# The product of Q with the carried state in 32x32 tiles into attention banks that ScalarE seeds, with statistics in steps and turns without loops

## What is computed

```
q = elu(x @ Wq.T + bq) + 1        # 16 heads of 32 features
k = elu(x @ Wk.T + bk) + 1
v = x @ Wv.T + bv
kv_cum = cumsum(k (outer) v, over tokens);  k_cum = cumsum(k)
out = (q . kv_cum) / max(q . k_cum, 1e-6)
y = out @ Wo.T + bo
...
second layer: blocks of 32 features scaled by their largest value and rounded
to an 8 bit grid, times the weight treated alike, + bias
```

## Time and profile before

| | us |
|---|---|
| median of 3 runs | 2538.85 (2538.05 to 2539.38) |
| the profiled execution | 2537.71 |
| its span, first to last instruction | 2535.9 |
| TensorE busy | 2475.8 (98%), 24082 records |
| VectorE busy | 2088.7 (82%) |
| ScalarE, GpSimd busy | 1139.3 (45%), 994.5 (39%) |
| TensorE's share of the chain that ended last | 86% |

### The profile page before, as it was taken

The page is one execution under the profiler, slowest core; times in us unless marked ns, Lnnn a source line. Parts: engine busy times, 40 slices in busy tenths (PEclk is TensorE's granted clock), DMA queues, the critical chain, the costliest instruction groups (busy, mean ns, idle before and its releaser), DMA issues.

```text
span 2535.9 us, 62336 instructions
## 1 busy us (share of the span) xinstructions
PE 2475.8 (98%) x24082; PEld 2058.8 (81%) x24082; DVE 2088.7 (82%) x4177; ACT 1139.3 (45%) x2058; POOL 994.5 (39%) x1482
## 2 busy tenths in 40 slices
PE   6999999999999999999999999999999999999996
PEld 4888888888888888888888888888888888888885
DVE  6888888888888888888888888888888888888875
ACT  4444445444444444454444454444444444544442
POOL 1233344343344343443433443434443334434334
PEclk8999999999999999999999999999999999999998
DMA  4011011110111110111110111101111101111001
GB/s 157 14 51 49 17 41 50 41 50 25 41 41 41 50 50 17 41 50 41 50 34 33 41 43 48 50 17 41 50 41 50 46 20 41 50 41 50 25 26 34
DMA packets 57483, 107.55 MB, mean 42 GB/s; under 512 B 6768, under 2 KB 7152, under 8 KB 56816
## 3 DMA queue, kind: packets, MB, share of 16 engines
q1 hardware_dynamic: 57456, 107.18, 12.8%
HBM read 73.60 MB, written 33.55 MB: 42 GB/s over the span
## 4 chain that ended last, share of the span: by engine, by line
PE 86%; DVE 8%; ACT 3%; issue 2%; DMA 1%; POOL 0%; DVEq 0%; POOLq 0%; SPq 0%
PE work L345 14%; PE work L347 13%; PE work L346 13%; PE score L345 9%; PE score L347 9%; PE score L346 9%; PE work L362 6%; PE score L436 4%; PE work L462 4%; DVE A L878 3%; PE work L455 2%; PE work L411 1%; PE state_bank L477 1%; ACT xn L599 1%; DVE oT_lo L885 1%
## 5 line engine op out<-in xcount | busy, mean ns | idle before, releaser
L878 DVE TENSOR_TENSOR A<-score,causal 128x512 f32<-128x512 f32 x512 | 316.8, 680 | 0.6 <-PE score L436 0.6
L1063 POOL TENSOR_TENSOR x_res<-x_res,o_buf 128x512 f32<-128x512 f32 x128 | 166.3, 1299 | 294.2 <-ACT o_buf L599 294.2
L1053 POOL TENSOR_TENSOR rs_f<-ve_f,minus_half 128x1 f32<-128x1 f32 x128 | 70.3, 549 | 419.8 <-DVE ve_f L797 419.8
L345 PE MATMUL work<-wv_hi,xT_hi 128*128 128x512 f32 x512 | 215.3, 420 | 0.0
L345 PE MATMUL score<-xT_hi,wq_hi 128*128 128x512 f32 x512 | 207.1, 404 | 7.3 <-DVE KT L816 7.3
L345 PE MATMUL score<-xT_hi,wk_hi 128*128 128x512 f32 x512 | 206.4, 403 | 6.2 <-issue 6.2
L345 PE MATMUL work<-wo_hi,oT_hi 128*128 128x512 f32 x512 | 202.7, 396 | 2.2 <-DVE oT_lo L885 1.9
L1072 POOL TENSOR_TENSOR xd<-q,xs 128x512 f32<-128x512 fp8e4 x128 | 148.3, 1159 | 137.6 <-PE work L362 137.6
L347 PE MATMUL work<-wv_hi,xT_lo 128*128 128x512 f32 x512 | 201.0, 393 | 0.0
L346 PE MATMUL score<-xT_lo,wq_hi 128*128 128x512 f32 x512 | 200.7, 392 | 0.0
L346 PE MATMUL work<-wv_lo,xT_hi 128*128 128x512 f32 x512 | 200.5, 392 | 0.0
(11 more groups left out here) (130 smaller groups left out, 6523.4 us busy)
## 6 DMA issues: line engine op xcount, KB each, us to landing
x_in<-in_x SPq DMA_DIRECT2D x128, 256.0 KB, 3.5
x_res<-in_x SPq DMA_DIRECT2D x128, 256.0 KB, 2.6
out<-f_buf SPq DMA_DIRECT2D x96, 256.0 KB, 2.0
out<-xd SPq DMA_DIRECT2D x32, 256.0 KB, 2.0
V<-in_wk SPq DMA_DIRECT2D x1, 1024.0 KB, 6.0
QT<-in_wq SPq DMA_DIRECT2D x1, 1024.0 KB, 7.5
kc<-in_wo SPq DMA_DIRECT2D x1, 1024.0 KB, 9.4
A<-in_wf SPq DMA_DIRECT2D x1, 1024.0 KB, 11.4
```

The costliest lines, as they stand in the source:

```text
L345: nc.tensor.matmul(dst, st_hi(c), mv_hi(c), start=(c == 0), stop=False)
L878: nc.vector.tensor_tensor(A[:, j, :, :], score_bank[j][:], causal[:].unsqueeze(1).to_broadcast([P, G, P]), ALU.mult).then_inc(a_set, 1)
L1053: nc.gpsimd.tensor_tensor(rs[n][:, b:b + 1], ve[n][:, b:b + 1], minus_half[:], ALU.pow).then_inc(rs_set[n], 1)
L1063: nc.gpsimd.tensor_tensor(x_res[:, b, :], x_res[:, b, :], o_buf[:, b % 2, :], ALU.add).then_inc(r_set, 1)
```

## The change

`attend` loses its four state matmuls. Instead `past_products` makes, once a turn after v(1), the product of Q with the state for all four b in 64 products of 32x32 weights: the rows of head j, the columns of group g, so 16 places of the array, into `score_bank[j]`. S now holds only the 32x32 blocks and is one copy a turn (`state` on ScalarE). ScalarE copies the four score banks into `past_att` (`past`), and writes for each b the att bank from it (`seed`), on which `attend` then accumulates. Heads in the attention output stand in another order, and the rows of Wo are laid out to match on the host. att is always in work bank 2. v(2) and v(3) now stand in front of the attention of b 0. The statistics are three functions (`x_seen` and its like, `join`, `widen`), as are the steps of quantise (`greatest`, `scale`, `quantise`), and stand apart with other work between; the carry copies are ScalarE's (`carry`). The loops are replaced by turns written out. ScalarE's, VectorE's and GpSimd's lists within a turn are reordered.

```diff
-    (("f", 2), W2), (("xd", 3), W1), (("den", 0), W0), (("v", 0), W2), (("kn", 0), W1), (("f", 3), W0),
-    (("v", 1), W1), (("x", 0), W2), (("att", 0), W0), (("kn", 1), W2),
-    (("v", 2), W1), (("o", 0), W2), (("x", 1), W0), (("att", 1), W1), (("kn", 2), W0),
-    (("v", 3), W2), (("o", 1), W0), (("x", 2), W1), (("att", 2), W2), (("kn", 3), W1),
-    (("x", 3), W0), (("o", 2), W1), (("att", 3), W0),
+    (("f", 2), W2), (("xd", 3), W1), (("v", 0), W0), (("den", 0), W2), (("kn", 0), W1), (("f", 3), W0),
+    (("v", 1), W1), (("v", 2), W2), (("v", 3), W0), (("x", 0), W1), (("att", 0), W2),
+    (("kn", 1), W0), (("o", 0), W1), (("x", 1), W0), (("att", 1), W2),
+    (("kn", 2), W1), (("o", 1), W0), (("x", 2), W1), (("att", 2), W2),
+    (("kn", 3), W0), (("x", 3), W1), (("o", 2), W0), (("att", 3), W2),
...
-        S = sb("S", [P, NSEQ, G, P])
+        S = sb("S", [P, NSEQ, G, DH])
+        past_att = sb("past_att", [P, NSEQ, HPG, P])
...
-            with sp.Fori(1, TILES - 1) as i:
+            for i in range(1, TILES - 1):
...
-                            pe.wait_ge(qn_set, count(i, 3))
+                            pe.wait_ge(past_set, count(i, HPG - 1))
...
-                def attend(b):
-                    if cur:
-                        take(i, ("att", b), here, before)
+                def past_products():
+                    if cur:
                         if first:
                             pe.wait_ge(state_zeroed, 1)
                         else:
-                            pe.wait_ge(s_set, count(i - 1, b))
-                        att = by_group(bank(("att", b))[:])
-                        for g in range(G):
-                            nc.tensor.matmul(att[:, g, :], S[:, b, g, :], QT[:, g, b * P:(b + 1) * P],
-                                             start=(g == 0), stop=False, skip_group_check=True)
+                            pe.wait_ge(s_set, count(i - 1, 0, 1))
+                        wait_apart(pe, qn_set, count(i, 3))
+                        for b in range(NSEQ):
+                            for g in range(G):
+                                for j in range(HPG):
+                                    rows = slice(j * DH, (j + 1) * DH)
+                                    last = nc.tensor.matmul(score_bank[j][g * DH:(g + 1) * DH, b, :], S[rows, b, g, :],
+                                                            QT[rows, g, b * P:(b + 1) * P], start=True, stop=True)
+                        last.then_inc(past_mm, 1)
+                def attend(b):
+                    if cur:
                         pe.wait_ge(a_set, count(i, b * HPG + HPG - 1, 16))
                         pe.wait_ge(v_set, count(i, b))
-                        for g in range(G):
-                            for j in range(HPG):
+                        pe.wait_ge(seeded, count(i, b))
+                        att = by_group(bank(("att", b))[:])
+                        for j in range(HPG):
+                            for g in range(G):
                                 feats = slice((g * HPG + j) * DH, (g * HPG + j + 1) * DH)
-                                last = nc.tensor.matmul(att[j * DH:(j + 1) * DH, g, :], V[:, b, feats],
+                                last = nc.tensor.matmul(att[g * DH:(g + 1) * DH, j, :], V[:, b, feats],
                                                         A[:, j, g, :], start=False, stop=True,
...
-                        if b > 0:
-                            pe.wait_ge(s_set, count(i, b - 1))
-                        elif not first:
-                            pe.wait_ge(s_set, count(i - 1, NSEQ - 1))
+                        if b == 0 and not first:
+                            pe.wait_ge(s_set, count(i - 1, 0, 1))
...
+                v(0)
                 denominators()
-                v(0)
                 kn(0)
+                f(3)
                 spread()
-                f(3)
+                v(1)
+                past_products()
+                v(2)
                 scores(0)
-                v(1)
+                v(3)
                 x_transposes(0)
                 attend(0)
                 state(0)
                 kn(1)
                 scores(1)
-                v(2)
                 if cur:
                     o(i, 0)
...
+                def carry(g):
+                    if cur:
+                        act.wait_ge(scanned, count(i, g))
+                        nc.scalar.copy(KT[:, g, :, CARRY], kc[:, g, :, SEG - 1]).then_inc(kc_set, 1)
...
-                def state(b):
-                    if cur:
-                        act.wait_ge(st_mm, count(i, b))
-                        for j in range(HPG):
-                            rows = slice(j * DH, (j + 1) * DH)
-                            last = nc.scalar.copy(S[rows, b, :, rows], state_bank[rows, b, :, :])
-                        last.then_inc(s_set, 1)
+                def past(j):
+                    if cur:
+                        act.wait_ge(past_mm, count(i, 0, 1))
+                        nc.scalar.copy(past_att[:, :, j, :], score_bank[j][:]).then_inc(past_set, 1)
+                def seed(b):
+                    if cur:
+                        take(act, i, ("att", b), {0}, set())
+                        if b == 0:
+                            act.wait_ge(past_set, count(i, HPG - 1))
+                        nc.scalar.copy(bank(("att", b))[:],
+                                       past_att[:, b, :, :].rearrange("p j t -> p (j t)")).then_inc(seeded, 1)
+                def state():
+                    if cur:
+                        act.wait_ge(st_mm, count(i, NSEQ - 1))
+                        nc.scalar.copy(S[:], state_bank[:]).then_inc(s_set, 1)
...
-            def stats(tile, n, b, src):
-                nc.vector.bn_stats(bn[n][:, b, :], src).then_inc(seen[n], 1)
+            def join(tile, n, b):
+                if n == "x" and not (isinstance(tile, int) and tile == 0):
+                    dve.wait_ge(rstd_set[n], count(tile - 1, b))
                 wait_apart(dve, seen[n], count(tile, b))
                 nc.vector.bn_aggr(mv[n][:, b, :], bn[n][:, b, :]).then_inc(joined[n], 1)
+            def widen(tile, n, b):
                 dve.wait_ge(joined[n], count(tile, b))
                 nc.vector.tensor_scalar(ve[n][:, b:b + 1], mv[n][:, b, 1:2], LN_EPS, None,
                                         ALU.add).then_inc(var_set[n], 1)
...
-                        dve.wait_ge(scanned, count(i, g))
-                        nc.vector.tensor_copy(KT[:, g, :, CARRY], kc[:, g, :, SEG - 1]).then_inc(kc_set, 1)
...
+    def by_head_in_group(w):
+        return np.ascontiguousarray(np.asarray(w).T.reshape(G, HPG, DH, D).transpose(0, 2, 1, 3).reshape(P, HPG, D))
```

More of the change, by code:

```diff
@@ L259, in had_before, with take @@
             return None
+        def take(engine, i, stage, here, before):
+            found = had_before(stage, here, before)
+            if found is None:
+                return
+            other, turns = found
+            reader, per = freed[other[0]]
+            engine.wait_ge(reader, count(i + turns + tile_of(other), other[1], per))
         def tokens(t, g):
@@ L333, in _ @@
         def _(pe):
[L334 to L341, removed]
             def product3(dst, st_hi, st_lo, mv_hi, mv_lo):
@@ L396, in v @@
                     if cur:
-                        take(i, ("v", b), here, before)
+                        take(pe, i, ("v", b), here, before)
+                        if first and b == 0:
+                            pe.wait_ge(wf_lo_set, G)
                         weights(i, "v")
@@ L402, in denominators @@
                     if cur:
-                        take(i, ("den", 0), here, before)
+                        take(pe, i, ("den", 0), here, before)
                         if first:
-                            pe.wait_ge(wf_lo_set, G)
                             pe.wait_ge(small_loaded, 16 * N_SMALL)
@@ L483, in x_transposes @@
                     if nxt:
-                        take(i, ("x", b), here, before)
+                        take(pe, i, ("x", b), here, before)
                         pe.wait_ge(xn_set, count(i + 1, b))
@@ L488, in o @@
                 def o(tile, b):
-                    take(i, ("o", b), here, before)
+                    take(pe, i, ("o", b), here, before)
                     pe.wait_ge(oT_set, count(tile, b))
@@ L495, in xd_transposes @@
                     if prev:
-                        take(i, ("xd", b), here, before)
+                        take(pe, i, ("xd", b), here, before)
                         pe.wait_ge(xd_set, count(i - 1, b))
@@ L501, in f @@
                     if prev:
-                        take(i, ("f", b), here, before)
+                        take(pe, i, ("f", b), here, before)
                         pe.wait_ge(xdT_set, count(i - 1, b))
@@ L573, in _ @@
             turn(0, {0, 1}, {1})
-            with pe.Fori(1, TILES - 1) as i:
+            for i in range(1, TILES - 1):
```

(56 more changed lines are left out.)

231 lines of the change are left out of this document (151 added, 80 removed).

## The result

The changed kernel takes **2466.7 us** (median of 4 runs, 2466.4 to 2468.8), the kernel before on the same chip 2538.5: ratio 0.972, 95% interval 0.970 to 0.974. The forecast was 2453, its range 2443 to 2490: right in sign and range, 13.7 us too low in size, and 0.7 us above its likeliest case (2444 to 2466), so in the first of its rivals (2466 to 2500). The profiled execution has a span of 2464.3 us, 71.6 less than before.

A forecast was written before the change was run, and what follows sets the result against it. TensorE's issue was taken as the bound. Per turn -4.18 + 1.25 + 0.55 = -2.38 us; 31 turns -73.8, branches -6.7, turn 0 -5.2, drain 0: -85.7 in all, from 2538.85 to 2453 us, range 2443 to 2490.

The forecast's parts named there:

- likeliest case: Whole kernel: 2444 to 2466 us, with the new group at 1.0 to 1.6 us; chance 0.75.
- first of its rivals: Some covers fail, or issue is slower with the new group at 1.9 us: 2466 to 2500 us; chance 0.14.
- Removed, 4.18 us a turn: TensorE no longer issues the four Q-times-state products in front of the attention matmuls: 4.18 us less per turn.
- The group at 1.25 us: The new group of 64 32x32 products, 128 records, was taken to add 1.25 us of TensorE time per turn.
- bound by columns in a tile (1.0): Lower bound for the new group: all 16 tiles side by side, 8 records in a row on each, 1.0 us.
- bound by rate of issue (1.36): New group's issue estimate: 127 steps of 9.1 ns, from the state product, plus 0.2 us to hand over: 1.36 us.
- Against the rule: New group: quartets on the same row groups overlap, against the skill's rule, which gives 3.6 to 4.4 us; that rival's chance 0.08.
- Change-overs, +0.55: TensorE switching between block kinds in the new order (v, o, x transposes, others): 0.55 us more per turn.
- Branches, -6.7: Writing the loop out removes TensorE's branch of 0.23 us, 29 times: 6.7 us less in all.
- Turn 0, -5.2: First turn saves 5.2 us: 2.4 from its terms, the QT wait of 2.6, and 0.2 for other waits.
- VectorE's part, "worth nothing but room": VectorE losing four carry copies and the statistics' stalls: no time gained, since VectorE isn't the bound.
- Covers: TensorE's new waits for QT, score copies, seeds and A stay hidden behind other work; QT's margin stays 0.37 us.

The follow-up runs named there:

- e12: Changed kernel with 32 instead of 128 moving columns in each of the 64 products of Q with the state: 2449.1 us, one run.
- e4: Changed kernel with 64 instead of 128 moving columns in each of the 64 products of Q with the state: 2455.9 us, one run.
- e5: Changed kernel with the two inner loops over the 64 products exchanged, so four in a row share their 32 rows: 2469.0 us.
- e10: Changed kernel with the row group as outermost loop over the 64 products, 16 in a row on the same 32 rows: 2492.7 us, one run.
- e2: Changed kernel with the 64 small products replaced by 16 of 128x128 weights, taken from KT instead of S: 2518.0 us.
- e1: Kernel before with its loop turns written out on all five engines, nothing else: 2531.5 us, ratio 0.9971.
- e6: Changed kernel with each sequence's 16 products taken along diagonals, so neighbours differ in rows, columns and bank: 2469.9 us.
- e7: Changed kernel with the split statistics alone undone, their steps again right behind each bn_stats; carry copies stay on ScalarE: 2488.9 us.
- e9: Changed kernel with the new group cut to its first sequence, 16 of the 64 products: 2424.0 us, one run.
- e11: Changed kernel with the group in two halves, sequences 2 and 3 moved behind the first two matmuls of v(2): 2481.4 us.

## Why the prediction was right, and 14 us too low

**Removed, 4.18 us a turn: right.** Its instructions are gone, and nothing waits in their place.

**The group at 1.25 us: the step that failed.** It is 1.83, 0.58 more: 18.6 us over 32 turns. The bounds came from good rows: with 32 columns, as in the state product's rows, records do start 8.6 ns apart (e12; 9.1 taken) and the group costs 1.21 us. But the group has 128 columns, and I took one value between the bound by columns in a tile (1.0) and the bound by rate of issue (1.36), below even the greater of the two. They add (e4, e12): 1.36 and the column time of the 96 columns that the state product doesn't have, some 0.6 (e12 to after), would have given 2.0, nearer to the truth, as the prediction's own 1.9 was, which it had put with the rival. Two of its signs of being right failed with this: the group at 1.0 to 1.6 us, and records at 8 to 12 ns (12.9).

**Against the rule: right for this order.** That quartets in the same four row groups run one after another, 3.6 to 4.4 us, did not come: 1.83. In e5 48 of 64 products follow one on their own rows, and the time is the same. e10, with 60 of 64, is dearer, 2.66, and its cause is open. The Trainium skill, "TensorE: Matmul & The Clock Gate", Part 3, would have a weight load wait for a running matmul on its own rows. The trace of after does not agree: the loads of the first 32 records start within 0.13 us, while one matmul record is listed with 0.29; e5 does not either, and e10 does not settle it. Its 10.6 times for 16 tiles is for 512 moving columns, which no run here has. By the trace, 64 dense products of 128 columns at the 0.218 us of e2 (3.49 / 16) would be 13.9 us, 7.6 times the 1.83.

**Change-overs, +0.55: nearly right.** The measured turns give +0.46 (75.08 - 76.97 + 4.18 - 1.83). In the two timelines the terms that the prediction lists are +0.35 (0.40 taken), +0.27 (0.24), +0.28 (0.27) and -0.29 (-0.36: the KT transposes, now before f(3), take 0.41 instead of 0.53, so give 0.12 and not 0.18), together +0.61. About 0.15 comes back where it lists nothing: in f(3) (2.95 to 2.91) and in the state groups of sequences 2 and 3 (0.47 and 0.46 to 0.41).

**Branches, -6.7: right** (e1: -7.4). **Turn 0, -5.2:** -5.3 measured with the dearer group in it, so -5.9 without; spread does wait for rden, 1.6 us, as said. That it fits so well is in part luck, since e5 and e6 reach turn 1 about 2 us later. **Drain: 0**, as said.

**VectorE's part, "worth nothing but room": wrong in its reason.** e7 shows what it pays for: 20 us. The prediction went through the waits for QT, the copies, the seed and A, but not through the work banks: in the new BANK_ORDER x(3) takes the bank of x(2), so its transposes wait for the xT_lo of sequence 2, which stands right behind o_buf and the statistics; before, x(3) took the bank of o(1). It did not ask what that cover would be without the split. It forecast no wait there, and there is none, because the split is part of the change. The sum came out unharmed, the attribution did not.

**Covers: right.** The quoted 0.37 us for QT stayed: in after it is written at 1265.06 + 2.48 = 1267.54, 0.39 before the group.

```profile
1265.06 2.48 DVE L919 TENSOR_TENSOR QT<-score,QT 128x512 f32<-128x512 f32 x4 [1.74 <-PE score L429]
```

**The sum:** the forecast span was 2450.2, and 2464.3 was measured, 14.1 more. Turns 1 to 30 saved 63.7 us where 78.1 were forecast (30 x 2.38 + 6.7), 14.4 less: per turn +0.58 for the group and -0.09 for the change-overs. The start saved 5.3 for 5.2, turn 31 and the drain 2.6 for 2.4. Of the rivals, "issue slower, 1.9 us, 2466 to 2500" is in truth the mechanism that came about, at its lower end; no cover failed.

## What to carry to other kernels

Take the price of a small matmul from rows with the same number of moving columns, and add the limits of issue and of columns rather than take the greater; a group of 16 or 32 small products was no bargain against one of 64 (27 and 31 ns a product against 29), and cutting a block of large ones for it cost 0.23 us. Where one engine is the bound, price another engine's saving by the first wait that would open without it: a margin of 0.85 us stood between 0 and 20 us here, and what a late buffer costs is more than the wait that the profile lists.

## What the runs showed of the hardware

- A wait of 0.19 us in TensorE's list cost 0.54 us of time: 0.26 before the four transposes and 0.28 in them, which took 0.69 instead of 0.41 (e7).
- The order of 64 products of 32x32 over 16 tiles made no difference in three orders that go through all 16 tiles before the first comes again: 1.83 us in after, e5 and e6; 16 in a row on the same rows cost 2.66 (e10).
- 16, 32, 64 such products: 0.43, 0.99, 1.83 us (e9, e11, after). The first 32 records start 7 ns apart but for one gap; from 32 products to 64 it is 26 ns a product.
- With 128, 64 and 32 moving columns the 64 products cost 1.83, 1.41 and 1.21 us (after, e4, e12).
- 30 turns written out on five engines, 3.5 MB of instructions, cost no wait in TensorE's steady turns (after); the loop's branch had cost it 0.2 us each time (e1).
